# A convolution, attention and mixture-of-experts block on one Trainium2 core: the expert number taken from a row register, and new hand-written orders

## The chip, the cores and the metric

The program runs on 1 core of one Trainium2 chip. The metric is the device time of the program in microseconds (us), median of several executions. All arrays are float32.

## The reference

Eight sequences of 375 tokens with 128 features pass through three stages; the second and third see a sequence of 373 after a max over windows of 3.

```python
# stage 1: convolutions 128 -> 64 -> 64 (3 taps) -> 128, layer norm, feed-forward 128 -> 64 -> 128, norm, max
h = silu(conv1(x)); h = silu(conv3(h)); h = conv1(h)
y = layer_norm(h + x)
y = layer_norm(gelu(y @ w_ff1.T + b) @ w_ff2.T + b + y)
h = max over y[t], y[t+1], y[t+2]
# stage 2: attention of one head; the values are the normed input itself
n = layernorm(h); q = (n @ Wq + bq) * 128**-0.5; k = n @ Wk + bk
h = h + softmax(q @ k.T) @ n
# stage 3: eight experts 128 -> 256 -> 128, each token weighted over its two best
n = layernorm(h); gates = softmax(relu(n @ gw1 + gb1) @ gw2 + gb2)
top_w, top_idx = top_k(gates, 2); top_w = softmax(top_w)
out = h + sum over the two e of top_w[e] * (gelu(n @ we1[e] + be1[e]) @ we2[e] + be2[e])
```

## The kernel before, in words

**Tiles.** A sequence of 375 tokens lies as 125 partitions x 3 tokens. Each step of a sequence is a named piece with a number, such as `a3.5` (third convolution of sequence 5), and each engine works through its own list of pieces, in exactly the order written out by hand: PE_ORDER (the number after the colon is the PSUM bank), DVE_ORDER (VectorE), ACT_ORDER (ScalarE), POOL_ORDER (GpSimd), SP_ORDER (SyncE, all of it DMA issues). Pieces that move something out of PSUM may stand in DVE_ORDER or in ACT_ORDER. Semaphores make each piece wait for its inputs, so an order decides what is queued behind a wait, not what is right.

**Stage 1.** `a1` (L1000), `a2` (L1011) and `a3` (L1049) are the convolutions. VectorE adds a3 to x (L729) and takes the statistics (L689, L693); GpSimd computes the reciprocal root in `p1` to `p4` (L516 to L525) and adds a row of biases to x in `xb` (L530); `l1` to `l4` apply the norm with three instructions each (L701 on VectorE, L566 on ScalarE). `a4` to `a7` are transposes and the feed-forward, `mp` is the max over windows. `ft`, `fn`, `cb` and `bf` prepare weights and biases once.

**Stage 2.** `hr` and `b1` transpose, `bq` makes the queries, `sc0` to `sc2` the scores, with the row maximum on VectorE (L822) and the exponential on ScalarE (L631), `pt0` to `pt2` transpose the probabilities, `at` multiplies (L1117) and VectorE adds and takes the statistics.

**Fillers.** The pieces `w.n` are matmuls of the identity with itself (L994) that compute nothing; WARM[n] says how many. One filler is two instructions in the trace.

**Stage 3, gates.** `g1` to `g3` (pairs of sequences) find the two best experts. For three pairs `rk` finds each token's rank among the tokens of its expert: the row is the expert's first row (CAP x e) plus the rank. The piece ends in `pos_x` (L895), the row numbers for the scatters.

**Stage 3, dense.** Sequences 0, 6 and 7 go through all eight experts: `D1` (L1174), gelu `dg` (L661), `D2` (L1181), and `da` (L923), which adds the weighted result on VectorE: 48 D1 and 24 D2. They depend on little and fill TensorE's gaps.

**Stage 3, sparse.** Sequences 1 to 5 are sorted by expert through DRAM. A buffer xs has room for CAP rows of 129 floats for each expert. SP first fills it from a blank tile (L415); thirty indirect DMAs `scat` on GpSimd (L543) write the normed rows there, and all of them must have landed before the first read. Then 37 blocks of 128 rows are worked through: the first 8 are block 0 of each expert, at a fixed row; for the other 29 (NDYN) a piece `cnt` on VectorE has made two tables in SBUF, tab_x with the first row of the block and tab_e with its expert. For a block n: `lx` on SP loads the 128 rows into one of 10 slots (L433 loads the row number from tab_x into a register, L434 issues the DMA); `lw` on SP copies the expert's weights and biases, 321 KB, from w_all in SBUF into one of 7 slots (L443 loads the expert number from tab_e, L444 issues), for n of 8 or more; `T` (L1190) transposes, `xT` evicts, `L1` (L1197), gelu `gl` (L672), `L2` (L1206), `yv` (L951) adds the bias and evicts, and `so` on GpSimd (L548) scatters the 128 result rows to ys. lx waits for the scatter of block n - 10 (L354), lw for the eviction of block n - 6 (L442). At the end SP reads ys back (`yl`, L453), VectorE combines in `fin` (L960, L964), and `out` and `od` write sequences out.

Blocks past the last used one read blank rows; the blank's last column makes the scatter of results skip them.

Of the kernel before, what the change touches and what calls it, by code (L numbers as in the profile page):

```python
# [67 lines left out]
b1.2:3 D1.0:6 bq.2:3 a7.5:1 sc0.2:3 sc1.2:4 h1.1:0 a4.7:7 sc2.2:1 b1.3:0 g1.0:2 bq.3:0 g2.0:2 sc0.3:0 sc1.3:3
sc2.3:7 pt0.2:1 hr.4:2 pt1.2:4 pt2.2:5 pt0.3:7 pt1.3:1 at.2:4 pt2.3:6 hr.5:7 a5.3:1 at.3:6 a6.6:2 rk.0:4 D1.1:1
D1.2:5 a6.7:6 h1.2:4 b1.4:7 h1.3:1 ct.0:3 bq.4:7 g1.1:1 sc0.4:7 g2.1:1 sc1.4:3 b1.5:5 sc2.4:4 D1.3:1 bq.5:5  # L70
sc0.5:5 sc1.5:3 a7.6:2 rk.1:7 sc2.5:0 a7.7:6 pt0.4:4 D1.4:5 pt1.4:2 pt2.4:7 pt0.5:0 pt1.5:2 pt2.5:6 at.4:7
at.5:6 hr.6:5 D1.5:2 hr.7:7 D1.6:5 bd.0:2 D1.7:6 D2.0:7 h1.4:1 h1.5:0 g1.2:0 b1.6:1 g2.2:0 D2.1:2 bq.6:0 b1.7:7
# [1178 lines left out]
```

## Time and profile before

| | us |
|---|---|
| median of 3 runs | 252.01 (250.09 to 252.61) |
| the profiled execution | 250.11 |
| its span in the trace | 248.4 |
| TensorE matmul busy | 220.9 |
| VectorE busy | 159.1 |
| ScalarE busy | 136.3 |
| GpSimd busy | 125.9 |

The span is what the trace covers; the profiled execution took 1.7 us more. All times of the trace are microseconds from the span's start. PE is TensorE's matmuls, PEld its weight loads, DVE VectorE, ACT ScalarE, POOL GpSimd, and SPq what SyncE's queue does: register work and the issuing of DMAs, which the page does not count as busy.

### The profile page before, as it was taken

The numbers are of one execution on the slowest core, as the hardware profiler recorded it, in microseconds if no ns is written. First come the engines' busy times: TensorE is split into PE (matmuls) and PEld (weight loads), VectorE is DVE, ScalarE is ACT, GpSimd is POOL, SyncE is SP. The second block draws the span as 40 slices with busy tenths as digits, with TensorE's granted clock in tenths as the row PEclk, the third lists the DMA queues.
The fourth block names the chain that finished last, engine by engine and source line by source line (L and its number), as shares of the span: only waits on it lengthen the run. The fifth ranks groups of instructions, "written<-read, shape, count | busy, mean of one in ns | idle before, by whom it ended". The sixth has DMA issues, their size and how long they took to land.

```text
span 248.4 us, 5630 instructions
## 1 busy us (share of the span) xinstructions
PE 220.9 (89%) x1621; PEld 176.2 (71%) x1621; DVE 159.1 (64%) x694; ACT 136.3 (55%) x303; POOL 125.9 (51%) x200
## 2 busy tenths in 40 slices
PE   7898999999999989989999887999799759989990
PEld 7565888778478646958569855888588459778780
DVE  0279699999997989898858463752322313215795
ACT  2235894977695769538982157644544323454510
POOL 8466556636303788888888416372633252643000
PEclk9999999999999999999999999999999997999998
DMA  5999999940100220112111255454536465620773
GB/s 132 248 250 298 352 393 390 393 162 0 31 3 1 52 55 22 44 44 73 45 47 45 55 170 198 144 174 153 203 120 254 148 215 192 223 70 13 206 220 91
DMA packets 28449, 36.81 MB, mean 148 GB/s; under 512 B 5387, under 2 KB 20036, under 8 KB 28419
## 3 DMA queue, kind: packets, MB, share of 16 engines
q1 hardware_dynamic: 24289, 32.25, 40.5%
q0 software_dynamic: 3680, 4.04, 6.0%
q8 instruction: 14, 0.23, 0.4%
q10 hardware_dynamic: 450, 0.16, 0.3%
q14 instruction: 16, 0.13, 0.2%
HBM read 10.61 MB, written 15.79 MB: 106 GB/s over the span
## 4 chain that ended last, share of the span: by engine, by line
POOL 21%; PE 20%; DVE 17%; SPq 14%; issue 12%; DMA 11%; ACT 3%; DVEq 0%; POOLq 0%; ACTq 0%
POOL xs L543 14%; DMA blk_x<-xs 5%; SPq L444 4%; POOL rstd L519 4%; SPq L443 3%; DVE stat L689 3%; PE PS L1206 3%; SPq L434 3%; DMA xt_sb<-in_xt 3%; PE PS L1197 3%; PE PS L1174 2%; SPq L433 2%; DVE x_sb L923 2%; DVE acc L960 2%; PE PS L1117 2%
## 5 line engine op out<-in xcount | busy, mean ns | idle before, releaser
L548 POOL DMA_INDIRECT ys<-yblk,blk_x x37 | 36.1, 975 | 46.7 <-DVE yblk L951 40.7
L543 POOL DMA_INDIRECT xs<-rows_x,pos_x x30 | 36.5, 1218 | 9.3 <-issue 9.0
L1174 PE MATMUL PS<-xt_sb,w_all 128*128 128x373 f32 x96 | 36.9, 485 | 1.2 <-ACT xt_sb L641 1.0
L1181 PEld LDWEIGHTS PS<-w_all,gd 128*125 128x125 f32 x288 | 34.4, 190 | 3.9 <-ACT gd L661 1.1
L1181 PE MATMUL PS<-w_all,gd 128*125 128x128 f32 x288 | 35.9, 276 | 0.5 <-ACT gd L661 0.4
L661 ACT ACTIVATE gd<-PS,bias 128x373 f32<-128x373 f32 x48 | 26.9, 573 | 17.1 <-PE PS L1174 14.4
L672 ACT ACTIVATE gb_t<-PS,blk_w 128x128 f32<-128x128 f32 x58 | 17.8, 366 | 28.0 <-PE PS L1206 20.4
L519 POOL TENSOR_TENSOR rstd<-ve,mhalf 125x3 f32<-125x3 f32 x32 | 27.9, 872 | 2.5
L516 POOL TENSOR_TENSOR ve<-mv,eps 125x3 f32<-125x3 f32 x32 | 6.4, 199 | 34.8 <-DVE mv L693 34.4
L951 DVE TENSOR_TENSOR yblk<-PS,blk_w 128x128 f32<-128x128 f32 x29 | 8.1, 286 | 24.4 <-PE PS L1206 22.6
L923 DVE SCALAR_TENSOR_TENSOR x_sb<-PS,comb,x_sb 125x128 f32<-125x128 f32 x72 | 20.7, 343 | 4.6 <-PE PS L1181 4.0
L1197 PE MATMUL PS<-xb_t,blk_w 128*128 128x128 f32 x116 | 18.5, 283 | 2.1 <-issue 1.5
L1174 PEld LDWEIGHTS PS<-xt_sb,w_all 128*128 128x128 f32 x96 | 15.4, 190 | 5.9 <-ACT xt_sb L641 1.4
L1197 PEld LDWEIGHTS PS<-xb_t,blk_w 128*128 128x128 f32 x116 | 15.7, 195 | 5.3 <-issue 3.5
L1099 PE MATMUL PS<-xn_t,q_t 128*125 128x373 f32 x48 | 18.1, 490 | 1.1 <-ACT q_t L625 1.1
L1190 PE MATMUL PS<-ident,blk_x 128*128 128x128 f32 x37 | 10.5, 289 | 9.3 <-DMA blk_x<-xs 9.3
L1206 PE MATMUL PS<-blk_w,gb_t 128*128 128x128 f32 x116 | 18.1, 286 | 0.0
L1117 PEld LDWEIGHTS PS<-xn,prob_t 125*125 125x125 f32 (+1 forms) x144 | 16.6, 187 | 1.7 <-issue 1.3
L808 DVE COPY xb_t<-PS 128x128 f32<-128x128 f32 x22 | 6.2, 287 | 18.0 <-PE PS L1190 11.3
L1117 PE MATMUL PS<-xn,prob_t 125*125 125x129 f32 (+1 forms) x144 | 17.6, 275 | 0.1
L1206 PEld LDWEIGHTS PS<-blk_w,gb_t 128*128 128x128 f32 x116 | 16.0, 201 | 0.8 <-ACT gb_t L672 0.3
L994 PE MATMUL PS<-ident 128*128 128x128 f32 x92 | 14.9, 318 | 1.7 <-POOL ident L475 1.7
(201 smaller groups left out, 444.1 us busy)
## 6 DMA issues: line engine op xcount, KB each, us to landing
xs<-blank SPq DMA_DIRECT2D x1, 9675.0 KB, 29.7
blk_w<-w_all SPq DMA_DIRECT2D x29, 321.0 KB, 2.5
blk_x<-xs SPq DMA_DIRECT2D x37, 64.5 KB, 1.9
yg<-ys SPq DMA_DIRECT2D x5, 336.0 KB
xt_sb<-in_xt SPq DMA_DIRECT2D x4, 375.0 KB, 6.7
x_sb<-in_x SPq DMA_DIRECT2D x4, 336.0 KB
out<-x_sb SPq DMA_DIRECT2D x8, 168.0 KB
w_all<-in_we SPq DMA_DIRECT2D x1, 1024.0 KB
```

The costliest lines, as they stand in the source:

```text
L519: pool.tensor_tensor(rstd[i][:, n % 2, :], ve[i][:, n % 2, :], mhalf[:], ALU.pow)\
L543: pool.indirect_dma_start(xs, bass.IndirectOffsetOnAxis(ap=pos_x[:, b // 2, s, i:i + 1], axis=0), rows_x[:, k, s, j, :], None).then_inc(s_ ...
L548: pool.indirect_dma_start(ys, bass.IndirectOffsetOnAxis(ap=blk_x[n % SLOTS][:, t, D:XW].bitcast(u32), axis=0), yblk[n % YBUF][:, t, :], No ...
L661: act.activation(gd[:, k % GD, c, 0:TP], of("D1", n)[:, 0:TP], ACT.Gelu, bias=bias128[:, 2 + k % E * HC + c:3 + k % E * HC + c]).then_inc( ...
L672: last = act.activation(gb_t[n % 2][:, c, :], of("L1", n)[:, c * BLK:(c + 1) * BLK], ACT.Gelu, bias=w[:, 2 * H + c:2 * H + c + 1])
L923: last = dve.scalar_tensor_tensor(flat(h2[:, b, :])[j], flat(of("D2", n)[0:P, :])[j], w[:, j, b % 2, e:e + 1], flat(h2[:, b, :])[j], ALU.m ...
L1099: pe.matmul(f[0:P, 0:TP], q_t[:, s, OFF[j]:OFF[j] + P], xn_t[:, s, :], start=True, stop=True)\
L1117: last = pe.matmul(f[0:P, j * (D + 1):(j + 1) * (D + 1)], prob_t[0:ROWS[c], s, c, OFF[j]:OFF[j] + P], xn3[0:ROWS[c], s, c, :], start=(c == ...
L1174: pe.matmul(f[:, 0:TP], w_all[:, k % E, c * 128:(c + 1) * 128], x32[:, DENSE[k // E], 0:TP], start=True, stop=True).then_inc(S["D1"], 1)
L1181: last = pe.matmul(f[0:P, j * D:(j + 1) * D], gd[:, n % GD, c, OFF[j]:OFF[j] + P], w_all[:, n % E, H + c * D:H + (c + 1) * D], start=(c == ...
L1197: last = pe.matmul(f[:, c * BLK:(c + 1) * BLK], w[:, c * 128:(c + 1) * 128], xb_t[n % 2][:], start=True, stop=True)
L1206: last = pe.matmul(f[:, t * D:(t + 1) * D], gb_t[n % 2][:, c, t * 128:(t + 1) * 128], w[:, H + c * D:H + (c + 1) * D], start=(c == 0), sto ...
```

## The change

It has five parts.

The expert's stretch of rows becomes CAP = 2048 (before 1920), a power of two, so a block's row divided by CAP is its expert. `lw` takes the register that `lx` of the same block has loaded and divides it; tab_e and its load are gone. In SP_ORDER each lw therefore stands behind its own lx. `cnt` drops the instruction for tab_e and clamps the row to the last block of xs with an instruction of its own. The rows past the experts (SPARE) are gone: xs has 16384 rows instead of 19200, and the fill writes 8256 KB instead of 9675, from a blank tile of 8 rows a partition instead of 6.

The fillers become 9 pieces of 29 in all, before 10 of 46. The input loads on SP are issued in another order. All five orders are rewritten: some evictions and norms change between VectorE and ScalarE.

```diff
-CAP = -(-T * NS // BLK) * BLK
-SPARE = E * CAP
-ROWS_X = SPARE + BLK * (1 + NDYN)
-KMAX = CAP // BLK - 1
+MOST = -(-T * NS // BLK)
+CAP = 2048
+assert MOST < CAP // BLK
+ROWS_X = E * CAP
+KMAX = MOST - 1
...
 PE_ORDER = """
-w.0:0 a1.0:0 w.1:1 a2.0:0 a2.1:1 ft.0:2 a1.1:3 a3.0:1 a3.1:0 cb.0:4 a2.2:2 a2.3:3 w.2:5 a1.2:1 a1.3:5 bf.0:1
+w.0:0 a1.0:0 w.1:1 a2.0:0 a2.1:1 w.2:2 cb.0:0 a3.0:1 a3.1:2 a1.1:0 w.3:3 bf.0:1 a2.2:0 a2.3:3 w.4:4 a1.2:2
...
-D1.35:7 L1.36:5 L2.35:3 D1.36:0 D1.37:5 L2.36:7 D2.16:0 D1.38:1 D2.17:5 D1.39:2 D1.40:1 D2.18:0 D1.41:2 D1.42:5
+L2.35:3 D1.36:2 L2.36:4 D1.37:0 D2.14:3 D2.15:1 D2.16:3 D1.38:1 D2.17:0 D2.18:2 D1.39:5 D1.40:1 D1.41:3 D2.19:5
...
 DVE_ORDER = """
-ft.0 a3.0 a3.1 cb.0 l1.0 bf.0 l1.1 a3.2 a3.3 l1.2 a6.0 a6.1 a3.4 l2.1 a3.5 mp.0 l1.4 hv.0 hr.0 fn.0 hr.1 l3.0
...
-l3.2 at.1 hv.3 hr.3 l4.1 l3.3 sc0.2 a4.6 sc1.2 mp.2 sc2.2 g2.0 sc0.3 sc1.3 sc2.3 g3.0 at.2 hv.4 hr.4 at.3 rk.0
-cw.0 l4.3 hr.5 a6.6 a6.7 l3.5 sc0.4 g2.1 sc1.4 g3.1 sc2.4 sc0.5 rk.1 sc1.5 sc2.5 pt0.4 pt1.4 pt2.4 pt0.5 mp.3
+cb.0 a3.0 a3.1 l1.0 l1.1 bf.0 a3.2 a3.3 ft.0 a6.0 a6.1 l2.0 l2.1 a3.4 mp.0 a3.5 hr.0 fn.0 hr.1 l3.0 a6.2 a3.6
...
+a6.5 sc0.2 l3.3 sc1.2 sc2.2 a7.4 h1.0 l4.1 pt0.2 a6.6 sc0.3 pt1.2 sc1.3 mp.2 sc2.3 at.2 g2.0 hr.4 g3.0 at.3 a6.7
+l4.3 hr.5 rk.0 cw.0 g1.1 sc0.4 sc1.4 g2.1 sc2.4 g3.1 sc0.5 pt1.4 rk.1 sc1.5 sc2.5 mp.3 at.4 hv.6 hr.6 at.5 l4.4
...
 POOL_ORDER = """
-p2.4 p4.0 p3.2 p2.5 p4.1 p3.3 p4.2 p3.4 p4.3 scat.0 scat.1 p3.5 scat.2 scat.3 p2.6 p2.7 scat.4 scat.5 scat.6
-scat.7 scat.8 scat.9 scat.10 p4.4 p4.5 p3.6 scat.11 p3.7 scat.12 scat.13 scat.14 scat.15 scat.16 scat.17 scat.18
+p4.0 p3.2 p2.4 p4.1 p3.3 p2.5 p2.6 p4.2 p3.4 p4.3 p2.7 p3.5 scat.0 scat.1 scat.2 scat.3 scat.4 scat.5 scat.6
+scat.7 scat.8 scat.9 p4.4 p3.6 p4.5 scat.10 scat.11 p3.7 scat.12 scat.13 scat.14 scat.15 scat.16 scat.17 scat.18
...
 SP_ORDER = """
-c4.1 c4.2 c4.3 c4.5 c4.4 lx.0 lx.1 lx.2 lw.8 lw.9 lx.3 lx.4 lx.5 lx.6 lw.10 lx.7 lw.11 lx.8 lw.12 lx.9 lx.10
-lw.13 lx.11 lx.12 lw.14 lx.13 lx.14 lw.15 lx.15 lw.16 lx.16 lw.17 lx.17 lx.18 lw.18 lx.19 lx.20 lx.21 lw.19
-lw.20 lx.22 lx.23 lw.21 lx.24 lx.25 lw.22 lw.23 lw.24 lw.25 lx.26 lw.26 lx.27 lx.28 lx.29 lw.27 lw.28 lw.29
...
+c4.1 c4.2 c4.3 c4.4 c4.5 lx.0 lx.1 lx.2 lx.3 lx.4 lx.5 lx.6 lx.7 lx.8 lw.8 lx.9 lw.9 lx.10 lw.10 lx.11 lw.11
+lx.12 lx.13 lw.12 lx.14 lw.13 lw.14 lx.15 lx.16 lw.15 lx.17 lw.16 lx.18 lw.17 lx.19 lx.20 lw.18 lw.19 lw.20
+lx.21 lx.22 lw.21 lw.22 lx.23 lx.24 lw.23 lx.25 lw.24 lw.25 lx.26 lx.27 lx.28 lw.26 lw.27 lw.28 lx.29 lx.30
...
-WARM = (11, 6, 6, 6, 4, 2, 2, 4, 2, 3)
+WARM = (5, 3, 4, 5, 1, 5, 2, 3, 1)
...
             load_x(sp, 0)
             load_xt(1)
             sp.dma_start(rows6[:], b_rows[:, 0:6 * D].rearrange("o (r d) -> (o r) d", d=D)).then_inc(S["rows6"], 16)
-            load_x(sp, 1)
             sp.dma_start(wf1_p[:], wf1).then_inc(S["wmid"], 16)
             for s in range(2):
                 sp.dma_start(wf2_p[HALF[s], s, :], wf2).then_inc(S["wmid"], 16)
-            load_xt(2)
-            load_xt(3)
+            load_x(sp, 1)
             for q in range(2, Q):
+                load_xt(q)
                 load_x(sp, q)
             sp.dma_start(gw1_p[:], gw1).then_inc(S["wt"], 16)
             for s in range(2):
...
+            row_of_block = {}
...
                     row = CAP * n if n < E else sp.value_load(tab_x[0:1, n - E:n - E + 1], min_val=0, max_val=ROWS_X - BLK)
+                    row_of_block[n] = row
                     sp.dma_start(blk_x[i][:], xs[bass.ds(row, BLK), :].rearrange("(p t) d -> p t d", t=NT))\
                         .then_inc(s_bx[i], 16)
...
-                    e = sp.value_load(tab_e[0:1, k:k + 1], min_val=0, max_val=E - 1)
-                    sp.dma_start(blk_w[k % WSLOTS][:], w_all[:, bass.ds(e, 1), :].rearrange("p o d -> p (o d)"))\
+                    sp.dma_start(blk_w[k % WSLOTS][:], w_all[:, bass.ds(row_of_block[n] // CAP, 1), :].rearrange("p o d -> p (o d)"))\
                         .then_inc(s_bw[k % WSLOTS], 16)
...
-                    dve.tensor_scalar(tab_e[:], eb[:], float(E - 1), None, ALU.min)
                     link(dve.tensor_tensor(adj_in[:], passed[:],
                                            stepx[0:1, :].unsqueeze(1).broadcast_to([1, NDYN, E]), ALU.mult))
                     link(dve.tensor_reduce(adj[:], adj_in[:], AX.X, ALU.add))
-                    dve.scalar_tensor_tensor(tab_x[:], block_no[0:1, :], float(BLK), adj[:],
-                                             ALU.mult, ALU.add).then_inc(S["tab"], 1)
+                    link(dve.scalar_tensor_tensor(adj[:], block_no[0:1, :], float(BLK), adj[:], ALU.mult, ALU.add))
+                    dve.tensor_scalar(tab_x[:], adj[:], float(ROWS_X - BLK), None, ALU.min).then_inc(S["tab"], 1)
```

## Rows read from the trace of the kernel before

**Rows 1.** Part 1 of the page: busy us, share of the span, instructions.

```profile
PE 220.9 (89%) x1621; PEld 176.2 (71%) x1621; DVE 159.1 (64%) x694; ACT 136.3 (55%) x303; POOL 125.9 (51%) x200
```

**Rows 2.** Windows: us, then busy and instructions of each engine, clock, DMA share.

```profile
13.50:82.20 68.70, 65.43 (x556) 50.95 (x557) 61.26 (x264) 49.15 (x101) 33.96 (x74) 1.00 0.61 200
82.20:120.50 38.30, 35.81 (x217) 25.83 (x216) 34.45 (x179) 26.32 (x52) 31.49 (x38) 1.00 0.21 50
...
140.60:225.40 84.80, 72.71 (x516) 61.48 (x515) 32.43 (x143) 40.45 (x118) 36.14 (x38) 0.98 0.50 168
225.40:248.40 23.00, 16.90 (x113) 13.75 (x111) 16.09 (x57) 5.73 (x10) 0.99 (x2) 0.95 0.49 143
```

**Rows 3.** Waits of TensorE, 140.5 to 225: us in total, times, longest.

```profile
PE PS L1190 <- DMA blk_x<-xs: 9.3, 8, 2.4
```

**Rows 4.** Waits of SP's queue, 140.6 to 225: us in total, times, longest.

```profile
SPq L434 <- DMA xs<-rows_x,pos_x: 28.2, 1, 28.2
SPq L443 <- DVE yblk L951: 0.3, 1, 0.3
```

**Rows 5.** The chain of waits, 165 to 200: start us, us, what.

```profile
181.58 0.63 PE PS L1174 x2
182.21 1.31 PE PS L1181 x12
...
187.41 0.30 SPq L443
187.75 0.15 SPq L443
...
188.10 0.49 SPq L444
```

**Rows 6.** SP's timeline: three row loads, and the last: start us, us.

```profile
192.98 2.64 SPq L434 DMA_DIRECT2D blk_x<-xs  x3
...
216.33 0.34 SPq L434 DMA_DIRECT2D blk_x<-xs  x1
```

**Rows 7.** GpSimd's timeline, scat.0 and scat.18: start us, us, [idle before].

```profile
84.23 1.33 POOL L543 DMA_INDIRECT xs<-rows_x,pos_x  x1 [0.80 <-issue]
...
120.77 1.19 POOL L543 DMA_INDIRECT xs<-rows_x,pos_x  x1 [0.31 <-DVE pos_x L895]
```

**Rows 8.** The chain of waits, the last scatter until it lands.

```profile
137.38 3.18 DMA xs<-rows_x,pos_x
```

**Rows 9.** VectorE's timeline: its first addition, and the third pos_x.

```profile
13.53 0.56 DVE L729 TENSOR_TENSOR r<-PS,x_sb 125x384 f32<-125x384 f32 x1 [1.25 <-PE PS L1049]
...
120.30 0.17 DVE L895 CAST pos_x<-pos 125x12 uint32<-125x12 f32 x1
```

**Rows 10.** Part 2 of the page: TensorE clock granted, 40 slices of 6.2 us.

```profile
PEclk9999999999999999999999999999999997999998
```

**Rows 11.** TensorE's timeline: a1.0 and a1.1 in the opening.

```profile
6.68 1.04 PE L1000 MATMUL PS<-xt_sb,wc_p 128*64 128x375 f32 x4
...
11.80 0.85 PE L1000 MATMUL PS<-xt_sb,wc_p 128*64 128x375 f32 x4 [1.03 <-DMA xt_sb<-in_xt]
```

**Rows 12.** GpSimd's timeline: xb.0 and xb.1 in the opening.

```profile
10.25 1.95 POOL L530 TENSOR_TENSOR x_sb<-x_sb,row_be 125x384 f32<-125x384 f32 x2 [3.44 <-DMA row_be<-in_b_rows]
```

**Rows 13.** VectorE by line: busy us, mean ns of one, idle before.

```profile
L701 DVE TENSOR_SCALAR xn<-h,mv,rstd 125x128 f32<-125x128 f32 x21 | 6.1, 344 | 1.5 <-POOL rstd L519 1.4
...
L828 DVE COPY prob_t<-PS 124x373 f32<-124x373 f32 (+1 forms) x8 | 4.0, 542 | 1.3 <-PE PS L1106 1.2
```

**Rows 14.** Part 6 of the page: the fill's issue, KB, us to landing.

```profile
xs<-blank SPq DMA_DIRECT2D x1, 9675.0 KB, 29.7
```

**Rows 15.** VectorE's timeline, its last pieces.

```profile
244.89 0.88 DVE L964 SCALAR_TENSOR_TENSOR x_sb<-yg,w_top,acc 125x128 f32<-125x128 f32 x3
```

**Rows 16.** Windows of the fillers (L994) alone: PE busy, PEld busy.

```profile
2.00:3.00 1.00, 1.00 (x6) 1.00 (x6) 1.00 0.67 119
8.00:9.00 1.00, 1.00 (x12) 1.00 (x10) 1.00 0.85 214
```

More of the change, by code:

```diff
@@ L68 @@
[L68 to L72, printed above, removed]
@@ new lines @@
+sc1.3:4 sc2.3:6 at.2:1 g1.0:0 hr.4:2 a7.6:5 g2.0:0 pt0.3:6 pt1.3:1 pt2.3:4 D1.0:2 hr.5:0 at.3:1 a6.7:4 h1.2:6
+b1.4:3 D1.1:7 rk.0:2 D1.2:3 bq.4:1 D1.3:0 h1.3:1 sc0.4:7 sc1.4:6 g1.1:1 sc2.4:4 g2.1:1 b1.5:3 bq.5:3 a7.7:7
+D1.4:6 pt0.4:4 pt1.4:3 sc0.5:1 pt2.4:4 sc1.5:2 rk.1:7 sc2.5:4 at.4:3 ct.0:7 pt0.5:4 pt1.5:2 pt2.5:1 hr.6:5
+at.5:1 D1.5:0 bd.0:7 D2.0:5 hr.7:6 D1.6:1 D1.7:3 h1.4:6 h1.5:2 b1.6:4 g1.2:6 D1.8:4 bq.6:7 g2.2:6 D1.9:5 b1.7:3
+D2.1:7 sc0.6:6 D2.2:1 D1.10:5 sc1.6:4 D1.11:2 rk.2:5 bq.7:3 cnt.0:0 sc2.6:5 sc0.7:3 sc1.7:6 D1.12:2 sc2.7:5
@@ new lines @@
+pt0.6:7 pt1.6:3 pt2.6:1 D2.3:4 pt0.7:5 pt1.7:3 D1.13:1 pt2.7:5 D1.14:7 D2.4:6 D2.5:0 at.6:3 at.7:5 D2.6:7
+D1.15:3 D2.7:3 h1.6:6 D1.16:6 h1.7:5 T.0:4 D1.17:1 T.1:7 T.2:4 L1.0:0 T.3:6 g1.3:5 L1.1:7 L2.0:0 L1.2:4 T.4:2
+L1.3:6 L2.1:0 T.5:4 T.6:2 L1.4:7 L2.2:3 L1.5:4 T.7:2 L2.3:6 L1.6:5 g2.3:2 T.8:6 L1.7:3 L2.4:4 L2.5:7 T.9:6
+D1.18:2 L1.8:7 D1.19:4 T.10:5 L2.6:0 L1.9:6 D1.20:3 L2.7:7 L2.8:5 L1.10:2 T.11:4 T.12:6 ct.1:0 D1.21:3 L2.9:2
+L1.11:4 T.13:7 D1.22:3 L2.10:5 T.14:6 bd.1:7 L2.11:4 L1.12:2 D1.23:0 L1.13:5 T.15:2 L2.12:6 T.16:1 D2.8:7
@@ new lines @@
+L2.13:6 T.17:5 L1.14:4 L1.15:2 D2.9:6 T.18:3 L2.14:4 L1.16:1 L2.15:2 D1.24:4 L2.16:1 T.19:2 L1.17:0 D2.10:7
+ct.2:0 L1.18:2 T.20:3 L2.17:5 T.21:6 L1.19:0 L2.18:3 T.22:5 L1.20:2 D1.25:0 L2.19:6 L1.21:2 D2.11:3 T.23:7
+L2.20:2 D1.26:0 T.24:6 L1.22:5 D1.27:4 L2.21:1 T.25:0 L1.23:3 T.26:7 L2.22:1 L1.24:6 D1.28:0 D2.12:1 L1.25:6
+L2.23:7 T.27:3 T.28:4 L2.24:5 D1.29:7 L1.26:0 D1.30:1 T.29:7 L2.25:5 T.30:3 L1.27:4 L2.26:0 L1.28:5 T.31:6
+D1.31:4 L2.27:0 L1.29:1 L1.30:5 T.32:0 L2.28:4 D1.32:1 D2.13:3 L2.29:6 T.33:4 L1.31:7 L1.32:5 L2.30:0 T.34:4
@@ new lines @@
+hv.0 hv.1 l1.4 a4.4 b1.0 l3.1 bq.0 b1.1 l2.2 sc0.0 sc1.0 sc2.0 a7.2 pt0.0 pt1.0 pt2.0 a7.3 a4.5 sc0.1 sc1.1
+sc2.1 a5.2 pt0.1 pt1.1 pt2.1 l1.6 l4.0 l1.7 b1.2 a4.6 a4.7 bq.2 l2.4 a5.3 sc0.2 b1.3 sc1.2 sc2.2 l2.5 bq.3 h1.1
+pt2.2 a7.5 sc0.3 l2.6 sc1.3 g1.0 sc2.3 hv.4 pt0.3 g2.0 pt2.3 pt1.3 l4.2 l3.4 dg.0 g3.0 b1.4 hv.5 a7.6 h1.2 bq.4
+dg.1 h1.3 l2.7 dg.2 l3.5 g2.1 b1.5 sc0.4 sc1.4 sc2.4 bq.5 pt0.4 g3.1 a7.7 pt2.4 sc0.5 sc1.5 sc2.5 pt0.5 pt1.5
+pt2.5 dg.3 ct.0 dg.4 hv.7 dg.5 h1.5 dg.6 b1.6 g1.2 dg.7 bq.6 g2.2 dg.8 dg.9 g3.2 dg.10 b1.7 dg.11 sc0.6 sc1.6
@@ new lines @@
+sc2.6 sc0.7 sc1.7 sc2.7 pt0.7 dg.12 dg.13 dg.14 dg.15 h1.6 xT.0 dg.16 h1.7 xT.1 gl.0 xT.3 gl.1 gl.2 dg.17 xT.5
+gl.3 gl.4 gl.5 g2.3 gl.6 dg.18 xT.9 gl.7 gl.8 xT.10 g3.3 dg.19 gl.9 dg.20 gl.10 dg.21 gl.11 xT.12 xT.13 gl.12
+gl.13 xT.15 gl.14 dg.22 gl.15 xT.17 gl.16 dg.23 xT.18 gl.17 gl.18 xT.20 gl.19 gl.20 dg.24 gl.21 dg.25 xT.22
+dg.26 gl.22 xT.24 xT.25 gl.23 gl.24 dg.27 dg.28 gl.25 dg.29 gl.26 xT.27 xT.28 gl.27 xT.29 dg.30 xT.30 gl.28
+dg.31 gl.29 xT.32 gl.30 gl.31 gl.32 dg.32 gl.33 gl.34 gl.35 gl.36 dg.33 dg.34 dg.35 dg.36 dg.37 dg.38 dg.39
```

59 lines of the change are left out of this document (19 added, 40 removed).

## The prediction

> **What bounds the kernel now.** I read the page's busy line first. TensorE is busy 220.9 of 248.4 us [rows 1]; no other engine passes 65%. So the first question is where TensorE's 27.5 us of idle lie. The windows give it [rows 2]. From 13.5 to 120.5 VectorE is the fullest engine in relation to the work that must follow (61.26 and 34.45 us busy of 68.7 and 38.3); TensorE idles 3.3 and 2.5 us there. From 140.6, when the first blocks can be read, to 225.4, when the last sparse block leaves PSUM, VectorE, ScalarE and GpSimd are all under half busy and TensorE still idles 84.8 - 72.7 = 12.1 us, at a granted clock of 0.98. That is nearly half of all its idle time.
>
> The waits of that stretch say for what. TensorE's transposes L1190 waited 9.3 us, 8 times, for the load of blk_x [rows 3]. The load was late though 10 slots are free to run ahead, so I look at who issues it. SP's own waits in the stretch are 0.3 us in all behind the first load [rows 4]: SP never waits for a slot or a block. It is the bound. The chain of waits shows the cadence: the weight copy issued at 188.10 is preceded by a table load and register work that begin at 187.41, and three row loads in a row take from 192.98 to 195.62, 1.16 us from one to the next [rows 5, 6]. SP needs 216.3 - 140.6, about 75.8 us, for its 37 row loads and 29 weight copies (the last row load is issued at 216.3 [rows 6], 9.1 us ahead of the last eviction at 225.4).
>
> Before that stretch GpSimd's thirty scatters set the time. They run without a gap at 1.49 us from 120.77 on, the one at 120.77 was released by VectorE's pos_x, and the last lands 3.18 us after 137.38 [rows 7, 8]. VectorE finished that pos_x at 120.30 + 0.17 [rows 9], so both engines tie at this point.
>
> Changes under about 1% can't be told from none for this kernel; my chances go by that.
>
> **The weight copy without its table load.** Gone for each of 29 copies: the TENSOR_LOAD (0.30 us in the row), a register step of 0.15, an assert and the gaps between: 187.41 to 188.00, 0.59 us; the 0.05 us register step ahead of the copy remains [rows 5]. Added: the division of the row register by 2048. No such step is in the trace. If it folds into the existing step it costs 0; the nearest row, the 0.15 us step at 187.75 with a gap of 0.04, gives 0.19. A chain of several such steps would be 0.6 and eat the whole gain. I take 0.10, between the first two. Net 0.49 us per copy, 14.2 us of SP in all (17 at best, 0 at worst). A copy then takes 1.23 - 0.49 = 0.74, a pair 1.9 instead of 2.4. The clamp of the row on VectorE replaces the table of experts: one instruction removed, one added, behind the last count, with nobody near in time: 0 (at most 0.2). The copy now always stands behind its own block's row load. Behind it on SP wait later row loads only, and copies need only the eviction 7 blocks before: 0, with 13 us of lead.
>
> **What becomes the bound there.** SP's 75.8 us becomes 61.6. TensorE's work in the same stretch was 72.7 us. In the new order D1.37, D2.14 and D2.15 come behind L2.36 instead of ahead of it: a D1 is 0.63 and a D2 1.31 [rows 5], so 0.63 + 2 x 1.31 = 3.3 us less. The clock of 0.98 over 84.8 us is worth 1.7 us; in the page's slices it falls in one place, the slice from 204.9 to 211.1 [rows 10], just behind the longest of the waits for blk_x, so I count 1.5 of it as won. That leaves 67.9 us, more than SP's 61.6. TensorE is the next bound. It won't be idle-free: from 13.5 to 120.5 it idled 5.8 of 107 us, 5.4%. 5.4% of 90 is 4.9, and the ramp at the first block adds something; I take 6.5 us of idle for the rest of the program, where 12.4 would be as before and 0 the least. So the gain here is 12.4 - 6.5 + 1.5 = 7.4 us.
>
> **The opening.** Before, eleven fillers held TensorE until a1.0 could start at 6.68, and a3.0 stood behind a1.1, which waited for its input until 11.80; VectorE's first addition came at 13.53 [rows 9, 11]. Now five fillers stand ahead and a3.0, a3.1 come before a1.1. GpSimd can't have the second row sum ready before 10.25 + 1.95 = 12.2 [rows 12], the first about 11.3. I let VectorE start at 12.2: 1.3 us earlier (between 0 and 2.2). The reduction of ft.0 (about 1.4 us), which lay in VectorE's idle start, now lies behind a3.3, in busy time: +1.4. Seventeen fillers fewer (46 to 29) free TensorE where it waits anyway: 0 (at most 17 x 2 x 0.083 = 2.8 us at the full rate of 12 instructions, two for a filler, in one us [rows 16], if all were in the way). The wf1, wf2 loads move ahead of the second x load; later x rows come about 1.5 us later, and TensorE needs them after the first pair is through: 0, at most 1.5.
>
> **Up to the last scatter.** Ahead of rk.2 on VectorE thirteen pieces leave and eleven come. Four of the leaving and three of the coming are normalisations of three instructions of 0.344; the others are evictions near 0.54 [rows 13]. (4 x 1.03 + 9 x 0.54) - (3 x 1.03 + 8 x 0.54) = 1.6 us less, or 1.5 with overlaps. VectorE's idle between 13.5 and 120.5 is 107 - 95.7 = 11.3; I leave it (a good new order might save 6, a bad one cost 3). pos_x of the third pair: 120.5 - 1.3 + 1.4 - 1.5 = 119.1.
> GpSimd: from 84.23 to 120.77 are 36.5 us, 18 scatters at 1.49 = 26.9 and seven norm pieces for 9.6. In the new order four of the seven remain in between, three (p2.6, p2.7, p3.5) come ahead of scat.0: 5.5. But rk.0 now stands behind a6.6, a6.7, l4.3 and hr.5, so VectorE gives pos_x for the first scatter some 3 us later: 87 + 26.9 + 5.5 = 119.4. Both engines tie again. I take 119.4 for scat.18, 1.4 us earlier, and so the first blocks at 139.2. Without the tie's help from either engine this is 0; with less idle on both it is 5.
>
> **The fill.** 16384 rows instead of 19200: 8256 KB for 9675. It landed 29.7 us after its issue [rows 14], near 54.5; it would be 4.4 us earlier. Its waiter is scat.0 at 84.23. Cover is 30 us: 0. The memset for it grows by about 0.2 us in a GpSimd idle of 3.44 [rows 12]: 0.
>
> **The end.** TensorE's work from the first blocks to its end was 72.7 + 16.9 = 89.6, now 88.1, with 6.5 idle: 139.2 + 94.6 = 233.8. Then two VectorE accumulations (1.9) and the output, 2.6 us from the last VectorE instruction (244.89 + 0.88) to 248.4 [rows 15]: 238.3. The sparse side: L2.36 at 139.2 + 72.7 - 3.3 - 1.5 + 6.5 = 213.6, and 23.0 us from the last eviction to the end as before: 236.6. SP's side: 139.2 + 61.6 + 9.1 + 23.0 = 232.9. The latest, 238.3, counts: 10.1 us less than 248.4. The profiled execution took 250.11, 1.7 above its span: 240.0. It is the low end of three runs with median 252.01; the same 10.1 off the median gives 241.9. I forecast 241.0.
>
> **Rivals.**
> 1. Part of SP's gain is not taken, because the new orders make new waits on TensorE (a block's transpose, copy, gelu and eviction in sequence) or weight copies land later at a higher rate. For it: TensorE's waits name one instruction before all, but two engines are near tie. Against: other engines are half idle there. With 12 us of idle instead of 6.5: 246.5.
> 2. Fewer fillers leave TensorE at its lower level when the real work begins. Between 2 and 3 us it finished 6 fillers, between 8 and 9 us 12 [rows 16], so it was at 1.2 GHz first and at 2.4 GHz later, after steady work. With five fillers it falls idle before a1.0; a1.0 and a2 (0.85 and 1.2 at full level) would take twice, +2.0 us, and the early start is lost: 241.0 + 2 = 243. The Trainium skill, page TensorE: Matmul & The Clock Gate, Part 1, says the array is cold by default and warms only under sustained activity; by that rule this rival happens, and the row agrees for the first fillers.
> 3. The arithmetic on the row register is about as dear as the load: 0.6 us. SP stays the bound, only the 1.4 us ahead of it and the tail's reorder remain: 250.
> 4. The other side: the division is lowered to a run of register steps, at 0.19 each six or more, 1.1 us. SP's copy gets 0.5 us longer, 29 x 0.5 = 14.5 us on the path: 252 - 1.4 + 14.5 = 265; it decides from 0.64 us of arithmetic (0.59 removed plus 1.4/29). For it: no such step is in the trace. Against: 2048 is a power of two, one shift, and one step of 0.05 already scales the number.
>
> **How the numbers follow.** Forecast (with rival 2 as its slow half) 0.76, of which rival 2 is 0.2; rival 1, 0.13; rival 3, 0.06; rival 4 or any loss in the attention stage 0.05. The fast end comes from 2 us of idle less, full folding and a VectorE that gains 3: 234. The slow end takes in rival 1: 247.5. Faster by over 1% (under 249.5): 0.90; within 1%: 0.06; slower: 0.04.
>
> **What would show it.** No TENSOR_LOAD on the copy's line, copies in a row 0.7 to 0.8 us apart, and SP waiting for evictions. TensorE's idle between the first block load and the last eviction under 7 us, and its wait at L1190 for blk_x under 4. Scatters from about 87 to 136, last landing near 139. A last eviction near 214 and no clock under 0.95 in between. It would be wrong if register steps fill the copy's gap, if SP still never waits, or if the scatters end after 141.

## The result and the profile after

| | before | after |
|---|---|---|
| median, us | 251.49 (250.09 to 252.61, 4 runs) | 239.77 (237.54 to 241.47, 4 runs) |
| the profiled execution | 250.11 | 237.54 |
| its span | 248.4 | 235.5 |

The ratio is 0.951 with a 95% interval of 0.942 to 0.960. The forecast was 241.0 us; for the profiled execution it was 240.0, and 237.54 came, the fastest of the four. Executions more than 1.5% above the fastest of their kernel are left out of all ratios, and of the medians of the experiments; the medians in this table are of all executions.

Parts 1 and 2 of the page after (against [rows 1, 10]): busy us of each engine, and the clock granted in 40 slices of 5.9 us.

```profile
PE 214.5 (91%) x1587; PEld 171.8 (73%) x1587; DVE 158.7 (67%) x686; ACT 137.8 (59%) x311; POOL 125.6 (53%) x202
...
PEclk9999999999999999999999999999999999999998
```

TensorE has 6.4 us less work in the records and 21.0 us idle instead of 27.5. The dip of the clock behind the waits is gone.

The windows after, same columns as [rows 2]; the third runs from the first block load past the last eviction.

```profile
13.50:82.20 68.70, 64.93 (x553) 49.78 (x553) 62.53 (x269) 53.89 (x108) 35.47 (x78) 1.00 0.58 186
82.20:120.90 38.70, 35.04 (x207) 25.18 (x206) 34.05 (x172) 26.93 (x55) 29.94 (x36) 1.00 0.19 46
141.10:213.90 72.80, 68.18 (x502) 59.16 (x503) 29.08 (x124) 38.90 (x119) 36.30 (x38) 1.00 0.59 195
213.90:235.50 21.60, 17.63 (x124) 14.82 (x122) 16.32 (x59) 7.34 (x14) 0.00 (x0) 0.96 0.52 151
```

VectorE's last eviction of a block:

```profile
211.44 0.29 DVE L950 TENSOR_TENSOR yblk<-PS,blk_w 128x128 f32<-128x128 f32 x1 [0.80 <-PE PS L1205]
```

It ends at 211.7, before at 225.4. Up to the first block load nothing was won: it is issued at 141.10, before at 140.6. All of the gain lies in the sparse stretch, which takes 70.6 us for 84.8. TensorE idles 72.80 - 68.18 = 4.6 us there, before 12.1.

The chain of waits after, 170.5 to 172.8: start us, us, what (against [rows 5]).

```profile
170.56 0.10 SPq L444
170.70 0.50 SPq L444
171.25 0.10 SPq L444
171.39 0.49 SPq L444
171.92 0.08 SPq L444
172.05 0.50 SPq L444
...
172.60 0.72 SPq L433
```

Three weight copies stand 0.69 and 0.66 us apart, before 1.23. Of a copy's register work one step of 0.10 is left, before 0.05: the division by 2048 cost 0.05 us. There is no table load on the copy's line.

SP's timeline after: the first and the last row load, and what SP does between and behind (against [rows 6]).

```profile
141.10 5.11 SPq L435 DMA_DIRECT2D blk_x<-xs  x9
...
201.06 1.09 SPq L464 DMA_DIRECT2D out<-x_sb  x2
202.20 0.42 SPq L466 DMA_DIRECT2D out<-x_sb  x1
203.63 0.38 SPq L435 DMA_DIRECT2D blk_x<-xs  x1
204.20 1.17 SPq L444 DMA_DIRECT2D blk_w<-w_all  x2
215.35 0.85 SPq L453 DMA_DIRECT2D yg<-ys  x2
```

The waits of SP's queue after, first those up to 180 us, then those from 206 to 214 (against [rows 4]; between 180 and 206 there is none): us in total, times, longest.

```profile
SPq L435 <- DMA xs<-rows_x,pos_x: 31.1, 1, 31.1
SPq L433 <- DMA ys<-yblk,blk_x: 2.2, 1, 2.2
```

```profile
SPq L354 <- DMA ys<-yblk,blk_x: 8.1, 2, 6.5
```

The second group is easily misread as SP having 8 us to spare. It comes after the last row load: it is the read-back of ys (L453) waiting for the last scatters. Between its first and last row load SP stood for 2.2 us of 62.5, ahead of the eleventh (lx.10), which waits for the result scatter of block 0. The list has no other wait of SP there: it is still nearly saturated.

TensorE's waits after, 141 to 214 (against [rows 3]).

```profile
PE PS L1189 <- DMA blk_x<-xs: 3.7, 4, 1.7
PE PS L981 <- DVE xn L701: 0.8, 1, 0.8
PE PS L1173 <- ACT xt_sb L641: 0.7, 1, 0.7
```

The opening after. TensorE's timeline (against [rows 11]):

```profile
4.72 1.52 PE L999 MATMUL PS<-xt_sb,wc_p 128*64 128x375 f32 x4 [0.54 <-DMA xt_sb<-in_xt]
6.17 1.65 PE L993 MATMUL PS<-ident 128*128 128x128 f32 x6
8.70 2.20 PE L1010 MATMUL PS<-hc,wm_d 64*64 64x192 f32 x24 [0.87 <-issue]
10.83 1.69 PE L993 MATMUL PS<-ident 128*128 128x128 f32 x8
12.45 0.22 PE L1018 MATMUL PS<-ident,rows 6*128 6x6 f32 x1
12.60 0.88 PE L1048 MATMUL PS<-we_d,hc 64*64 64x128 f32 x24
```

VectorE's first addition and third pos_x (against [rows 9]):

```profile
13.55 0.56 DVE L729 TENSOR_TENSOR r<-PS,x_sb 125x384 f32<-125x384 f32 x1 [0.61 <-PE PS L1048]
...
120.94 0.17 DVE L895 CAST pos_x<-pos 125x12 uint32<-125x12 f32 x1
```

a1.0 starts 1.96 us earlier than before, and nothing comes of it: a1.0, a2.0 and the fillers run at half speed (a2's 24 instructions take 2.20; at 15.72 in the same trace the same 24 take 1.21), and `cb.0` (L1018) stands at 12.45 in front of a3.0. VectorE starts its first addition at 13.55, before at 13.53.

GpSimd's timeline, scat.0 and scat.18 (against [rows 7]):

```profile
88.58 1.33 POOL L543 DMA_INDIRECT xs<-rows_x,pos_x  x1 [0.79 <-issue]
...
121.41 1.19 POOL L543 DMA_INDIRECT xs<-rows_x,pos_x  x1 [1.39 <-DVE pos_x L895]
```

The fill lands 25.8 us after its issue by part 6 of the page, before 29.7 [rows 14].

### The profile page after: what moved, and what is told of

Read it like the earlier page. It is cut to its first block, busy times and chain, and to the rows that moved or that the text cites. A ratio compares the mean times of both kernels' runs of the same rounds, so it can differ in the third digit from the quotient of the medians.

```text
span 235.5 us, 5477 instructions
## 1 busy us (share of the span) xinstructions
PE 214.5 (91%) x1587; PEld 171.8 (73%) x1587; DVE 158.7 (67%) x686; ACT 137.8 (59%) x311; POOL 125.6 (53%) x202
## 4 chain that ended last, share of the span: by engine, by line
PE 26%; DVE 23%; POOL 14%; issue 13%; SPq 12%; DMA 8%; ACT 2%; DVEq 0%; POOLq 0%; ACTq 0%
POOL xs L543 10%; SPq L433 4%; SPq L444 4%; DVE stat L689 4%; SPq L435 3%; DMA blk_x<-xs 3%; DMA ys<-yblk,blk_x 3%; PE PS L1098 3%; POOL rstd L519 3%; PE PS L981 3%; PE PS L1173 2%; PE PS L1196 2%; PE PS L1205 2%; DVE x_sb L923 2%; DVE acc L959 2%
## 5 line engine op out<-in xcount | busy, mean ns | idle before, releaser
L1173 PE MATMUL PS<-xt_sb,w_all 128*128 128x373 f32 x96 | 37.6, 485 | 1.3 <-ACT xt_sb L641 0.7
L1180 PEld LDWEIGHTS PS<-w_all,gd 128*125 128x125 f32 x288 | 33.6, 187 | 3.7 <-ACT gd L661 1.3
L1180 PE MATMUL PS<-w_all,gd 128*125 128x128 f32 x288 | 34.7, 273 | 0.8 <-ACT gd L661 0.8
L1098 PE MATMUL PS<-xn_t,q_t 128*125 128x373 f32 x48 | 18.8, 494 | 0.5 <-DVE q_t L816 0.4
L1196 PE MATMUL PS<-xb_t,blk_w 128*128 128x128 f32 x116 | 17.4, 277 | 0.0
L631 ACT ACTIVATE prob<-PS,nmax 125x373 f32<-125x373 f32 x24 | 12.6, 577 | 4.0 <-DVE nmax L822 3.9
L822 DVE TENSOR_REDUCE nmax<-PS 125x1 f32<-125x373 f32 x24 | 12.4, 541 | 1.1 <-PE PS L1098 0.9
## 6 DMA issues: line engine op xcount, KB each, us to landing
xs<-blank SPq DMA_DIRECT2D x1, 8256.0 KB, 25.8
```

Of the source, the lines that this page charges most:

```text
L1098: pe.matmul(f[0:P, 0:TP], q_t[:, s, OFF[j]:OFF[j] + P], xn_t[:, s, :], start=True, stop=True)\
L1173: pe.matmul(f[:, 0:TP], w_all[:, k % E, c * 128:(c + 1) * 128], x32[:, DENSE[k // E], 0:TP], start=True, stop=True).then_inc(S["D1"], 1)
L1180: last = pe.matmul(f[0:P, j * D:(j + 1) * D], gd[:, n % GD, c, OFF[j]:OFF[j] + P], w_all[:, n % E, H + c * D:H + (c + 1) * D], start=(c == ...
L1196: last = pe.matmul(f[:, c * BLK:(c + 1) * BLK], w[:, c * 128:(c + 1) * 128], xb_t[n % 2][:], start=True, stop=True)
```

## The experiments

They ran in three groups, each on one chip with the kernel before beside it. Its median was 259.24 us beside e1 to e4, 251.53 beside e5 to e8 and 257.63 beside e9 to e12, so times are compared within a group, and across groups only as ratios to the kernel before. e5 and e12 are the changed kernel itself. Behind each median stands how many executions it is taken from. A ratio is not the quotient of two such medians and differs from it by up to 0.5%.

| run | median, us (executions) | ratio to before, 95% |
|---|---|---|
| e1 register alone, old engine orders | 253.06 (3 of 4) | 0.981 (0.973 to 0.988) |
| e2 new orders, table load kept | 259.47 (7 of 10) | 0.999 (0.994 to 1.004) |
| e3 kernel before, new SP order | 261.56 (7 of 10) | 1.007 (1.002 to 1.012) |
| e4 changed kernel, 7 more early fillers | 248.25 (4) | 0.955 (0.949 to 0.961) |
| e5 changed kernel | 238.75 (4) | 0.949 (0.943 to 0.955) |
| e6 e4, and the bias transpose later | 237.21 (4) | 0.945 (0.938 to 0.952) |
| e7 changed kernel, 14 slots | 238.71 (4) | 0.949 (0.941 to 0.956) |
| e8 changed kernel, 14 table loads back | 246.72 (4) | 0.983 (0.976 to 0.990) |
| e9 changed kernel, row numbers as constants | 245.36 (4 of 5) | 0.953 (0.947 to 0.959) |
| e10 changed kernel, old size of xs | 247.43 (2 of 4) | one round |
| e11 e6 with 14 slots | 242.67 (2 of 6) | 0.942 (0.934 to 0.950) |
| e12 changed kernel | 249.25 (3 of 4) | 0.969 (0.961 to 0.977) |

### Which part gives the gain: e1 to e4

**e1**: the register, CAP and the smaller fill, with the new SP order (every lw behind its lx). PE, DVE, ACT and POOL orders, fillers and input loads are those of before.

```diff
-PE_ORDER, DVE_ORDER, ACT_ORDER, POOL_ORDER, WARM, input loads: new
+PE_ORDER, DVE_ORDER, ACT_ORDER, POOL_ORDER, WARM, input loads: as before
```

> The register, the 2048 rows and the smaller fill alone: engine orders, fillers and input loads are those of before; the SP order is the new one, since each copy must stand behind its own row load. Theory 1 (SP's issue rate was the bound, the register frees it): first block loads near 140.6 as before, copies in a row 0.70 us apart, last eviction near 214 to 218, time 242 to 245 against 251.5. Theory 2 (the new engine orders bring the gain, the register only moves SP's load): 249 to 252, and TensorE idle from first load to last eviction still near 12 us.

**e2**: everything new, but the expert number is again loaded from its table.

```diff
-sp.dma_start(blk_w[k % WSLOTS][:], w_all[:, bass.ds(row_of_block[n] // CAP, 1), :]
+e = sp.value_load(tab_e[0:1, k:k + 1], min_val=0, max_val=E - 1)
+sp.dma_start(blk_w[k % WSLOTS][:], w_all[:, bass.ds(e, 1), :]
...
+dve.tensor_scalar(tab_e[:], eb[:], float(E - 1), None, ALU.min)
```

> The changed kernel with the expert number loaded from its table again (one TENSOR_LOAD, one 0.15 us register step and an assert per copy, 0.55 us more for each of 29 copies, 16 us of SP's time), all new orders kept. Theory 1: SP is the bound again, last eviction 8 to 12 us later than 211.7, time 247 to 251. Theory 2: time 240 to 242, as SP waited 8.7 us for slots in the changed kernel and could give that.

**e3**: the kernel before with nothing new but SP_ORDER.

> The kernel before with only the new order of SP's row loads and copies. Theory 1: SP does the same work at the same rate, 2.4 us a pair, so 250 to 253; the ramp may shift by 1 us as nine row loads now stand ahead of the first copy. Theory 2 (order of SP counts): 247 or less.

**e4**: the changed kernel with one more filler ahead of a1.0 and six more ahead of a2.0.

```diff
-WARM = (5, 3, 4, 5, 1, 5, 2, 3, 1)
+WARM = (6, 9, 4, 5, 1, 5, 2, 3, 1)
```

> The changed kernel with 6 fillers for 5 ahead of a1.0 and 9 for 3 ahead of a2. Theory A (the early matmuls run at 1.2 GHz because the fillers are too few): a2 takes 1.2 us instead of 2.2, VectorE's first addition comes at 12.0 to 12.5 instead of 13.55, and if VectorE's start carries through, the first block loads come 1 us sooner and the time falls to 238.5 to 239. Theory B (the opening is hidden: the third pos_x depends on later waits): first addition earlier, time unchanged at 239.8 within 0.5.

Measured: e3 261.56, e2 259.47, e1 253.06, e4 248.25. With the old orders the register is worth 261.56 - 253.06 = 8.5 us, with the new ones 259.47 - 248.25 = 11.2. The new orders without the register are worth 261.56 - 259.47 = 2.1, with it 253.06 - 248.25 = 4.8. Together (e4) they give 13.3; the 2.7 us above the sum are hardly more than the intervals. The changed kernel itself was not in this group; e4 stands for it, and differs by its fillers. The new SP order alone costs 0.7%. e2 came as theory 1 said. e1 came as neither: 0.981 of 251.5 is 246.7, between the two ranges, and its last eviction ends at 226.0 instead of 214 to 218.

That the orders can't do it without the register is read from TensorE's waits: first e2, 142 to 235, then e1, 142 to 226.

```profile
PE PS L1191 <- DMA blk_x<-xs: 9.2, 10, 2.0
```

```profile
PE PS L1198 <- ACT xb_t L668: 2.5, 1, 2.5
PE PS L1207 <- DVE yblk L952: 1.7, 1, 1.7
PE PS L1166 <- DVE comb_t L806: 1.1, 1, 1.1
...
PE PS L1191 <- DMA blk_x<-xs: 0.6, 1, 0.6
```

With the table load, TensorE waits for blocks as before, 9.2 us, whatever its order is. With the register and the old orders it waits little for blocks (0.6), but for copies and evictions of other engines. These waits are not what the new orders take away. The windows of e1 and then of e4, each from the first block load to the last eviction and from there to the end, columns as in [rows 2]:

```profile
142.48:226.01 83.53, 75.27 (x540) 64.01 (x540) 32.51 (x143) 39.98 (x118) 36.10 (x38) 0.98 0.52 170
226.01:249.70 23.69, 16.70 (x114) 13.71 (x112) 16.13 (x58) 5.73 (x10) 1.02 (x2) 0.93 0.47 139
```

```profile
143.16:223.54 80.38, 71.22 (x490) 60.32 (x489) 29.73 (x131) 38.53 (x118) 35.32 (x38) 0.96 0.53 177
223.54:247.90 24.36, 20.10 (x142) 16.93 (x140) 17.29 (x62) 7.79 (x14) 1.73 (x2) 0.96 0.47 135
```

In the stretch TensorE idles 8.3 us in e1 and 9.2 in e4, no less. e4's stretch is 3.1 us shorter because it holds less work, 71.2 us for 75.3: D1.37, D2.14 and D2.15 stand behind L2.36 in the new order. They come where TensorE idled: its idle behind the last eviction is 7.0 us in e1 and 4.3 in e4. The two profiled executions differ by 1.8 us only (e1's is its fastest, e4's its slowest), the medians by 4.8; what else the orders give is not traced.

SP's waits in e1 look like time to spare:

```profile
SPq L435 <- DMA ys<-yblk,blk_x: 6.9, 2, 6.4
```

They are not. The long one stands ahead of lx.10, and SP stands there in every profile of this group, 5.0 us in e3, which has all its table loads, 6.0 in e2 and 5.3 in e4. It belongs to the new SP order and to how late block 0's results land, not to what the register freed. My first reading of e1, that SP now had much slack in the changed kernel too, was wrong, as the second group shows.

### Is SP still on the path: e5, e7, e8

**e5** is the changed kernel again, **e7** gives it 14 slots for rows instead of 10.

```diff
-SLOTS = 10
+SLOTS = 14
```

**e8** puts the table load back for every second copy: 14 of 29 (the expectation says 15).

```diff
+e = sp.value_load(tab_e[0:1, k:k + 1], min_val=0, max_val=E - 1) if k % 2 else row_of_block[n] // CAP
```

> The changed kernel itself, on the same chip as the three below and with its own runs of before. Both theories: ratio 0.945 to 0.96 to before. It is the base of the other three.

> The changed kernel with 14 slots for row blocks instead of 10, so that SP's waits for the result scatter of block n - 10 (8.7 us in the changed kernel) go away. Theory 1 (TensorE is the bound of the sparse stretch now, 68 of 73 us busy): within 1 us of the changed kernel, at most 1.5 faster. Theory S (SP's chain still sets the stretch through these waits): 3 us or more faster.

> The changed kernel with the expert number loaded from its table for the odd block numbers only: 15 of 29 copies carry the 0.55 us again, 8 us of SP's time. The full 29 cost 11.8 us. Theory 1 (TensorE is the bound in the changed kernel, SP has slack): convex, so clearly less than half, 1 to 4 us over the changed kernel. Theory S (SP still sets the pace in the changed kernel): linear, 6 us over it.

Measured: e5 238.75, e7 238.71, e8 246.72. By the times slots are worth nothing; SP waits for one only 2.2 us. In the two profiled executions the stretch is 69.4 us with 14 slots and 70.9 with 10, so at most 1.5 us can be in it. e8 costs 8.0 us for 14 loads, against 14 x 0.59 = 8.3 us of SP time by [rows 5]. So nearly every SP microsecond put back in is on the path; with real slack the first loads would have been free, as theory 1 said. Theory 1 falls. e8's waits, of SP ahead of its last row load, then of TensorE:

```profile
SPq L433 <- DMA ys<-yblk,blk_x: 1.1, 1, 1.1
```

```profile
PE PS L1191 <- DMA blk_x<-xs: 6.3, 5, 2.3
```

Its last row load is issued at 211.83, 70.5 us behind the first at 141.36, against 62.5 us in the changed kernel: 7.9 us more, the whole loss. e8's page also shows the dip of the clock again that the changed kernel had lost, behind a wait of 1.6 us for blk_x; the 7.9 us leave little for it.

```profile
PEclk9999999999999999999999999999999589999999
```

### Fewer fillers and the bias transpose: e6

**e6** takes e4's fillers and moves `cb.0`, the transpose of the bias rows, behind a3.0 and a3.1 on TensorE and VectorE.

```diff
-w.2:2 cb.0:0 a3.0:1 a3.1:2 a1.1:0
+w.2:2 a3.0:1 a3.1:2 cb.0:5 a1.1:0
...
-cb.0 a3.0 a3.1 l1.0
+a3.0 a3.1 cb.0 l1.0
...
-WARM = (5, 3, 4, 5, 1, 5, 2, 3, 1)
+WARM = (6, 9, 4, 5, 1, 5, 2, 3, 1)
```

> The changed kernel with more early fillers (6 and 9 for 5 and 3) and cb.0, the transpose that waited for the 3 KB load of the bias rows until 12.5, behind a3.1 instead of ahead of a3.0 (PSUM bank 5). Theory A (the opening is on the path): a3 starts near 11.0, VectorE's first addition near 12.2, all of stage 1 a good 1 us earlier, and the changed kernel's time falls by 1 to 1.5 us. Theory B (slack is absorbed before the third pos_x): first addition near 12.2 but the scatter that waits for pos_x and the time stay within 0.5 us.

Measured 237.21, 1.5 us under e5; the two intervals overlap, so by the times this is unclear. The timelines are not. TensorE in the opening, first e4, then e6, and VectorE's first addition and third pos_x in e6:

```profile
8.80 1.21 PE L1010 MATMUL PS<-hc,wm_d 64*64 64x192 f32 x24
...
12.53 0.22 PE L1018 MATMUL PS<-ident,rows 6*128 6x6 f32 x1 [1.44 <-DMA rows<-in_b_rows]
```

```profile
8.47 1.21 PE L1010 MATMUL PS<-hc,wm_d 64*64 64x192 f32 x24
...
10.85 0.88 PE L1048 MATMUL PS<-we_d,hc 64*64 64x128 f32 x24
```

```profile
11.85 0.56 DVE L729 TENSOR_TENSOR r<-PS,x_sb 125x384 f32<-125x384 f32 x1 [10.30 <-POOL x_sb L530]
...
119.26 0.17 DVE L895 CAST pos_x<-pos 125x12 uint32<-125x12 f32 x1
```

With more fillers a2.0 runs at full speed, and it then shows what stood behind the slow a2.0: the 3 KB load of the bias rows, for which cb.0 waits until 12.53. In e4 that alone holds a3.0, so e4 wins nothing at this place: VectorE's first addition stays at 13.64, where theory A had 12.0 to 12.5. With cb.0 out of the way a3.0 starts at 10.85 and the first addition at 11.85, 1.7 us earlier than after. The lead lasts to the first block load: pos_x 119.26 for 120.94, and the load at 139.4 for 141.1. Against after it is gone by the last eviction, 211.6 for 211.7; SP takes 64.9 us from first to last row load there instead of 62.5. Against e5, on the same chip, the last eviction is 3.3 us earlier, but e5's profiled execution is its slowest (241.11) and has the fall of the clock told of below. So theory A holds up to the first block load; what it is worth in time isn't shown here.

### Constants for row numbers, the fill, both together: e9 to e12

**e9** uses the row numbers that the tables hold for this input as constants, so that a row load needs no table load and a copy no arithmetic. It leaves out the reading of the table, and so holds for this input alone.

```diff
-row = CAP * n if n < E else sp.value_load(tab_x[0:1, n - E:n - E + 1], min_val=0, max_val=ROWS_X - BLK)
+row = CAP * n if n < E else KNOWN[n - E]
```

> The changed kernel with the row numbers of the 29 later blocks written into the program for this input, so that SP loads no table and does no register arithmetic at all: a row load and a weight copy then cost SP about 0.9 us together instead of 1.85, some 27 us of SP's time less. The table on VectorE is still made. Theory 1 (TensorE is the bound of the stretch now): at most 2 us faster than the changed kernel, with TensorE's idle in the stretch near 3 us. Theory S (SP still sets the pace, as the 15 table loads that cost 8 us suggest): 3 to 6 us faster, limited only by TensorE's idle of 4.6 us there.

**e10** gives xs its old 19200 rows; the clamp stays at the changed kernel's last block.

```diff
-ROWS_X = E * CAP
+ROWS_X = 19200
```

> The changed kernel with xs of 19200 rows again (9675 KB of fill from a blank tile of 6 rows), the rows in use as in the changed kernel. All theories: the fill lands near 54 instead of 50, 30 us ahead of its waiter, so the time is the same within 0.5 us.

**e11** is e6 with e7's 14 slots, **e12** the changed kernel on this chip.

> The changed kernel with the faster opening (fillers 6 and 9, cb.0 behind a3.1) and 14 slots for row blocks. Theory A (the opening carries through to the first block load): 1 to 2 us faster than the changed kernel, first block load near 139.5; the slots alone brought nothing and should add nothing.

> The changed kernel, as the base of the three beside it on the same chip. Ratio to before 0.945 to 0.955.

Measured: e12 249.25, e9 245.36, e10 247.43, e11 242.67. e12 itself missed its expectation (0.945 to 0.955) with 0.969; the last section comes back to it. e9 takes 3.9 us off, within theory S's 3 to 6, though it takes some 27 us of register work off SP: in after two row loads in a row are issued 1.15 us apart and the issue itself takes 0.35, which leaves 0.80 for each of 29, and 0.14 for each of the 27 copies ahead of the last row load. So SP was still worth something, and most of those 27 us met the next bound. e9's one profile is of an execution of 251.03 us, 5.7 above its median, and is used below for its opening alone. e10's larger fill lands 30.3 us after its issue instead of 25.0 in e12; no cost of it is seen, as far as two executions tell. e11 is 6.6 us under e12, more than the 1 to 2 expected, and its interval is clear of e12's, though only two of its six executions count. In the profiles of the two, pos_x comes at 121.06 for 123.99, the last eviction at 219.7 for 223.1 and the end at 244.4 for 247.2: the faster opening's 2.9 us last to the end there. What the rest of the 6.6 is, and whether the slots have a part in it on this chip, was not tried.

## Why the prediction was right, and where it was not

**The copy without its table load: right.** I took 0.49 us off a copy; it is 1.23 - 0.69 = 0.54. For the division I took 0.10 and it cost 0.05. SP's span from first to last row load was to be 61.6 and is 62.5, with 1.6 us of output issues in it (201.06 to 202.62) that I hadn't counted and 2.2 of waiting. That it is so near has another reason: I took the gain of 29 copies off, but in the new SP_ORDER lw.35 and lw.36 stand behind the last row load. Those two (1.4 us) and 0.05 us more for each of 29 made up for most of the 3.8.

**"TensorE is the next bound": wrong step, though it cost little.** I set 67.9 us of TensorE's work against SP's 61.6. But the first runs to the last eviction and the second only to the last row load, which is 9.1 us ahead of it. Like for like it was 67.9 against 61.6 + 9.1 = 70.7. Measured are 211.7 - 141.1 = 70.6 (the last eviction is 8.1 us behind 203.63). I had SP's figure, and took TensorE's 67.9 + 6.5 = 74.4 over it. SP stayed the bound or tied with it: TensorE waited 3.7 us for blocks (under 4 was foreseen), e8 put 8.0 us back for 8.3 of SP work, and e9 took 3.9 off for 27. Work put in on SP costs one for one, work taken out gives a seventh: that is a tie. "SP waiting for evictions", which I named as a sign, hardly happened (2.2 us for a slot, none for an eviction).

**The rest of the idle: oversized.** 6.5 us were taken for the rest of the program. TensorE ends at 231.5 now, 90.4 us after the first block load, with 68.18 + 17.63 = 85.8 busy: 4.6 idle. Its busy time was to be 88.1; it is 2.3 less. Behind TensorE's end I counted 4.5 us, and 4.0 came. In sum the part behind the first block load took 235.5 - 141.1 = 94.4 instead of 99.1, so 4.7 us better.

**The opening and the scatters: the gain didn't come.** VectorE was to start at 12.2 and the first block load to be issued at 139.2; they came at 13.55 and 141.1, so 1.9 us worse. From first addition to third pos_x I had 106.9 us, and 120.94 - 13.55 = 107.4 came: the count of pieces on VectorE held. What failed is "I let VectorE start at 12.2", where I looked at GpSimd's row sum alone. Two things stood ahead of it. One is rival 2, at its place: a1.0 took 1.52 and a2.0 2.20 instead of 0.85 and 1.21. The other I hadn't seen: cb.0 and the load it needs. e4 removes the first and stays at 13.6; e6 removes both and has 11.85. With e6's opening pos_x came at 119.26 and the first block load at 139.4, where I had 119.1 and 139.2. The tie of VectorE and GpSimd didn't hold either: GpSimd stands 1.39 us ahead of scat.18 for pos_x. And one of my signs of being wrong came: the last scatter starts at 137.92 and the first block load, which waits for its landing, is issued at 141.10, so the scatters end just behind 141 and not near 139.

The two errors, +1.9 and -4.7, leave 2.8 us: span 238.3 forecast, 235.5 measured. They have opposite signs, so that the sum came out so near is in part luck.

**At nothing: right.** The fill's size has no cost that e10 can show. The SP order, forecast at 0, costs 0.7% with the table load in (e3), where SP stands 5.0 us ahead of lx.10; with the register it wasn't tried alone.

**Rivals 3 and 4 fell** at the 0.05 us step. Rival 1's 12 us of idle didn't come: 4.6 in after. But on the two other chips it comes nearer, 9.2 us in e4 and 78.90 - 69.39 = 9.5 in e12. The waits that it spoke of are seen with the old orders too (e1, at TensorE 2.5 + 1.7 + 1.1 us), where the idle is 8.3, so they don't explain why e1 stops at 0.981.

## What to carry over

When a queue's span is set against an engine's work, both must be measured between the same two events: a queue's last issue lies ahead of the engine's last piece, here by 8 to 9 us. Before a wait is read as slack, see which instruction waits: 8.1 us of SP's waits belonged to the read-back behind the stretch, and e1's 6.4 stood there with the table loads in, too. No wait in the list doesn't mean none: look for breaks in the queue's timeline (e12, below). A load that is small and early in the program can still land late; a piece that needs it belongs behind the pieces that don't.
